# A two-layer transformer kernel: where ScalarE's exponential, roundings and one copy stand in a key-tile loop, and shifts written by four instructions

## The chip, the cores and the metric

The kernel runs on one core of one Trainium2 chip. The metric is device time in microseconds of one execution; the kernel before took 3008.36 us in the median of three runs. TensorE is PE in the profile (PEld is its weight load), VectorE DVE, ScalarE ACT, GpSimd POOL, and SP issues the loads.

## The reference, cut to what matters

Two layers run over x, 32 examples of 64 tokens by 256, with a context of 1601 rows by 256 for each example. Each layer is a cross attention, a self attention and a feed-forward part. The change touches only the second layer's two attentions:

```
kv = (mem @ W_kv).reshape(B, Nkv, 2, HEADS, HEAD_DIM)
k = kv[:, :, 0].transpose(0, 2, 1, 3)
v = kv[:, :, 1].transpose(0, 2, 1, 3)
q = (x @ W_q).reshape(B, Nq, HEADS, HEAD_DIM).transpose(0, 2, 1, 3)
attn = jnp.einsum('bhqd,bhkd->bhqk', q, k) * SCALE
attn = jax.nn.softmax(attn, axis=-1)
out = jnp.einsum('bhqk,bhkd->bhqd', attn, v)
...
return out @ W_proj + b_proj
```

with 16 heads of 16 columns. Then comes a causal self attention with the same heads, computed for two examples (128 tokens) at a time:

```
scores = jnp.where(causal, scores, NEG_INF)
attn = jax.nn.softmax(scores, axis=-1)
out = jnp.einsum('bhst,bhtd->bhsd', attn, V)
...
return scrambled @ W_O
```

## The kernel before, in words

The program goes through four stages: the first layer's attentions (up to some 370 us), its quantized feed-forward part (up to some 625 us), the second layer's attentions (from there to some 2485 us, called the stage here), and an expert feed-forward part. The change lies in the stage.

**Pairs and examples.** The stage runs over 16 pairs of examples. TensorE's program is unrolled over them; ACT, DVE, POOL and SP run the 14 inner pairs as a loop. In pe_batch each example n of a pair has two phases.

*Maxima and projections.* The largest score of each head is needed before any exponential. TensorE makes rounded scores of the example's keys in 16 units (maxima, L1167; unit 0 to 15, two units for each of 8 head pairs), and DVE reduces each to a maximum (L1677). A unit waits until the unit two before it is reduced. Between the units TensorE projects the next example's context to keys (8 pieces, L1145 to L1147) and values (7 pieces, L1154 to L1156), in float32 split into a rounded part and its rest, three products each. ACT copies each key piece out twice, raw and rounded (L780, L781), and POOL subtracts (L550). Behind unit 0 stands the last key tile's weighing of the example before (weigh, L1179), which closes its sums; ACT copies them to SBUF (copy_sums, L835), and behind unit 2 TensorE spreads the denominators (end_batch, L1188), from which DVE takes reciprocals and divides (L1666, L1668). Then the 16 maxima are transposed (L1301), DVE makes two bfloat16 parts of the negated maxima (L1683, L1685) and writes shift, a block pattern on four groups of 8 partitions (L1693), while TensorE does the last three value pieces. The first score matmul (L1317) adds shift and waits for all four groups.

*Scores.* 13 tiles of 128 keys (the last has 65). TensorE makes exact scores of tile t (L1317, L1321) in one of two PSUM halves, ACT takes exponentials (L853), and TensorE weighs the values with them two tiles later, two tiles together (L1179). Tile t waits for the exponentials of tile t - 2.

**What is woven in.** During the scores of a pair, the self attention of the pair before is done beside them, in pieces named by places: place t is tile t of example 0, and place PLACES + t (PLACES is 14) is tile t of example 1. The self attention's 16 heads go in four quarters of four heads. For quarter q TensorE makes scores (L1222), DVE adds the mask, takes maxima and centres (L1702, L1708, L1710), ACT exponentiates (exp_p4, L799), TensorE transposes (L1231), ACT copies the transposed ones out (copy_p4T, L803), TensorE weighs (L1243), DVE copies (L1723), and TensorE transposes back (L1251). The tables S4_AT, EXP_P4_AT, COPY_P4T_AT, P4T_AT, O4_AT and O4T_AT give each quarter's place on its engine. The order on each engine is this hand-written one; an engine that waits holds up everything behind.

ACT also rounds the context of the next example but one (round_ctx, L793), in four parts of 128 x 801 at the tiles of CTX_AT, and POOL makes the rest of each (split_ctx, L558). ctx_raw, the buffer of the raw context, holds half an example's columns (parts 0 and 1, or parts 2 and 3). SP loads the next half (L394) when POOL has finished the two parts of the half before. At tile 7 of example 1, behind parts 2 and 3, ACT copies the normalized x of the next pair (copy_xnT, L691), which TensorE's queries need (L1272, place QUERY_AT[1]).

## Time and profile before

| | us |
|---|---|
| median of 3 runs | 3008.36 (3006.55 to 3012.42) |
| the profiled execution, device time | 3009.89 |
| its span, first to last instruction | 3007.8 |
| PE busy | 2529.8 (84%) |
| PE weight loads busy | 2148.3 (71%) |
| DVE busy | 1612.2 (54%) |
| ACT busy | 1336.3 (44%) |
| POOL busy | 903.5 (30%) |

All rows come from the profiled execution. In a timeline a row is one or several like instructions in order: start, length, engine, line, operation, output<-input, shapes, count, and in brackets the engine's idle time ahead of it with what ended it. A busy PE is a modelled one (matmuls overlap), so where it matters the starts of its rows are compared rather than their ends. "issue" as the end of a wait means that the profile shows nothing that the engine waited for.

### The profile page before, as it was taken

To read this page: it belongs to the slowest core of one execution; us is meant where nothing else is said; L and a number is where in the kernel's file an instruction comes from. 1 tells how busy PE (TensorE), PEld (TensorE's weight loads), DVE (VectorE), ACT (ScalarE), POOL (GpSimd) and SP (SyncE) were. 2 spreads that over 40 slices of the span, in tenths; PEclk is the share of its full clock that TensorE was granted. 3 is DMA by queue.
4 is the path that set the end of the run, shared out by engine and by line. 5 is a ranking of instruction groups with operands and counts; after the bars stand their busy time and mean duration, and the time that the engine had idled before them with its cause. 6 is when DMAs were issued, how large, how long until landed. Compare 5 with 4: busy or idle time off the path is not lost.

```text
span 3007.8 us, 75415 instructions
## 1 busy us (share of the span) xinstructions
PE 2529.8 (84%) x32180; PEld 2148.3 (71%) x32180; DVE 1612.2 (54%) x2741; ACT 1336.3 (44%) x2115; POOL 903.5 (30%) x868
## 2 busy tenths in 40 slices
PE   6999823248999999999999999999999973699997
PEld 3555511137888878888888888888888743699997
DVE  3434377724446456456455455455555543477775
ACT  1212211124555555555555555555555421456564
POOL 1000024344333433442442442443443203211121
PEclk9999955569999999999999999999999975799999
DMA  8888600031010110110110110101101002466664
GB/s 342 323 314 311 235 0 0 0 110 45 24 46 23 35 35 23 35 35 23 35 35 23 35 35 27 43 24 34 35 24 35 2 1 100 159 212 209 209 208 147
DMA packets 48438, 270.05 MB, mean 90 GB/s; under 512 B 4881, under 2 KB 23442, under 8 KB 33554
## 3 DMA queue, kind: packets, MB, share of 16 engines
q1 hardware_dynamic: 40018, 255.69, 23.4%
q0 software_dynamic: 8160, 10.29, 2.2%
q8 instruction: 237, 3.88, 0.5%
q14 instruction: 23, 0.19, 0.0%
HBM read 247.45 MB, written 20.61 MB: 89 GB/s over the span
## 4 chain that ended last, share of the span: by engine, by line
PE 68%; issue 11%; DVE 10%; ACT 6%; POOL 2%; DMA 2%; SPq 0%; ACTq 0%; POOLq 0%; DVEq 0%
PE PS L1321 8%; PE PS L1179 7%; PE PS L1167 5%; PE PS L1317 3%; PE PS L1051 3%; DVE shift L1693 3%; PE PS L1145 3%; PE PS L1147 3%; PE PS L1146 3%; PE PS L1031 3%; PE PS L1408 3%; PE PS L1409 3%; PE PS L1410 3%; PE PS L1156 2%; PE PS L1154 2%
## 5 line engine op out<-in xcount | busy, mean ns | idle before, releaser
L1677 DVE TENSOR_REDUCE mpart<-PS 128x1 f32<-128x802 f32 (+1 forms) x512 | 487.7, 987 | 366.4 <-PE PS L1167 365.1
L853 ACT ACTIVATE probs<-PS 128x1024 f32<-128x1024 f32 (+1 forms) x416 | 413.7, 1026 | 242.2 <-PE PS L1321 242.1
L550 POOL TENSOR_TENSOR k_lo<-probs,k_hi 128x400 fp32r<-128x400 f32 (+1 forms) x256 | 255.7, 999 | 305.0 <-ACT k_hi L781 305.0
L558 POOL TENSOR_TENSOR ctx_lo<-ctx_raw,ctx_hi 128x801 fp32r<-128x801 f32 x128 | 221.8, 1750 | 359.4 <-ACT ctx_hi L793 350.8
L1321 PE MATMUL PS<-qbd_hi,k_hi 64*128 64x256 f32 (+1 forms) x1664 | 313.4, 373 | 0.0
L1167 PE MATMUL PS<-k_hi,qbd_hi 128*128 128x512 f32 (+2 forms) x1024 | 263.3, 359 | 22.4 <-POOL ctx_lo L558 14.2
L780 ACT COPY probs<-PS 128x400 f32<-128x400 f32 (+1 forms) x256 | 126.5, 494 | 305.7 <-PE PS L1147 305.7
L1179 PE MATMUL PS<-probs,vals 128*32 128x64 f32 x13312 | 233.8, 221 | 5.7 <-issue 5.6
L1154 PE MATMUL PS<-wkv_hi,ctx_hi 128*128 128x256 f32 (+1 forms) x832 | 236.4, 284 | 0.0
L1321 PE MATMUL PS<-qbd_lo,k_hi 64*128 64x256 f32 (+1 forms) x1664 | 234.5, 278 | 0.0
L1321 PE MATMUL PS<-qbd_hi,k_lo 64*128 64x256 f32 (+1 forms) x1664 | 234.4, 278 | 0.0
L1156 PE MATMUL PS<-wkv_hi,ctx_lo 128*128 128x256 f32 (+1 forms) x832 | 234.3, 282 | 0.0
L1155 PE MATMUL PS<-wkv_lo,ctx_hi 128*128 128x256 f32 (+1 forms) x832 | 233.2, 280 | 0.0
L1179 PEld LDWEIGHTS PS<-probs,vals 128*32 128x32 f32 x13312 | 196.7, 110 | 45.2 <-issue 28.6
L1167 PEld LDWEIGHTS PS<-k_hi,qbd_hi 128*128 128x128 f32 x1024 | 178.4, 192 | 46.6 <-DVE mpart L1677 24.7
L1408 PE MATMUL PS<-xT_hi,unit_hi 128*128 128x256 f32 x736 | 209.0, 284 | 1.7 <-DVE xT_lo L1920 1.7
L1409 PE MATMUL PS<-xT_lo,unit_hi 128*128 128x256 f32 x736 | 209.3, 284 | 0.0
L1410 PE MATMUL PS<-xT_hi,unit_lo 128*128 128x256 f32 x736 | 208.7, 284 | 0.0
L783 ACT COPY vals<-PS 128x512 f32<-128x512 f32 x192 | 113.0, 589 | 214.3 <-PE PS L1156 214.3
L1145 PE MATMUL PS<-ctx_hi,wkv_hi 128*128 128x400 f32 (+1 forms) x512 | 186.9, 365 | 18.7 <-POOL ctx_lo L558 18.7
L1317 PE MATMUL PS<-shift,onesb 64*128 64x512 bf16 (+1 forms) x832 | 163.8, 390 | 23.5 <-DVE shift L1693 13.5
L664 POOL DMA_INDIRECT sum_d<-scaled,xg x46 | 75.8, 1648 | 346.5 <-DVE scaled L1957 339.5
(322 smaller groups left out, 6088.8 us busy)
## 6 DMA issues: line engine op xcount, KB each, us to landing
unit_raw<-in_experts SPq DMA_DIRECT2D x46, 1536.0 KB, 7.1
ctxN<-in_ctxN SPq DMA_DIRECT2D x16, 3328.0 KB, 10.8
ctxT<-in_ctxT SPq DMA_DIRECT2D x16, 3204.0 KB, 10.4
ctx_raw<-in_ctxT SPq DMA_DIRECT2D x64, 801.0 KB, 4.5
slots_d<-pad_rows SPq DMA_DIRECT2D x2, 2990.0 KB, 18.7
xg<-slots_d SPq DMA_DIRECT2D x23, 260.0 KB, 2.8
x<-in_x SPq DMA_DIRECT2D x1, 2048.0 KB, 9.6
sum_d<-x SPq DMA_DIRECT2D x1, 2048.0 KB, 6.3
```

Of the source, the lines that this page charges most:

```text
L550: g.tensor_tensor(k_lo[:, n, a, c:c + width], k_raw[p % 2][:, 0:width], k_hi[:, n, a, c:c + width].bitcast(F32), ALU.subtract).then_inc(s. ...
L853: act.activation(probs[rows, t % PROBS, :], PS[rows, 1024 * (t % 2):1024 * (t % 2) + 1024], ACT.Exp).then_inc(s.pr_ready, 1)
L1145: pe.matmul(bank(at, width), wkv_hi[:, k, cols], ctx_hi[:, k, c:c + width], start=k == 0, stop=False)
L1154: pe.matmul(to, ctx_hi[:, k, keys], wkv_hi[:, k, D:2 * D], start=k == 0, stop=False)
L1156: mm = pe.matmul(to, ctx_lo[:, k, keys], wkv_hi[:, k, D:2 * D], start=False, stop=k == KT - 1)
L1167: mm = pe.matmul(at, qbd_hi[:, n, pair // 4, (pair % 4) * P:(pair % 4) * P + P], k_hi[:, n, pair // 4, c:c + width], start=True, stop=True)
L1179: mm = pe.matmul(bank(4, S, slice(32 * j, 32 * j + 32), g * S), vals[rows, n, mine:mine + 32], probs[rows, t % PROBS, at_head(h):at_head(h ...
L1321: mm = pe.matmul(bank(2 * (t % 2) + r, 256, rows, a * 256), keys_part[part, n, a, keys], queries[part, n, a, r * 256:r * 256 + 256], start ...
L1408: pe.matmul(to, hi[:, k, cols], tokens_hi[:, k, :], start=k == 0, stop=False)
L1409: pe.matmul(to, hi[:, k, cols], tokens_lo[:, k, :], start=False, stop=False)
L1410: mm = pe.matmul(to, lo[:, k, cols], tokens_hi[:, k, :], start=False, stop=k == KT - 1)
L1677: v.tensor_reduce(mpart[:, pair, half:half + 1], PS[:, at:at + width], AX, ALU.max).then_inc(s.mx_red, 1)
```

## The change

ACT's order in the score loop changes at three points, and DVE's shift instructions are joined. (1) The third quarter's exponential is put at tile 11, in front of the last tile's exponential, instead of behind it; so that the second quarter's copy of transposed exponentials (also at tile 11) does not fall behind it, copies are now issued ahead of exponentials where both stand at one tile. (2) Parts 0 and 1 of the context rounding stood together behind tile 1; part 1 now stands behind tile 3. (3) The copy of the sums stood behind the evacuation of key piece 0 and now stands ahead of it. (4) The shift is written by four instructions of 8 x 512, one for each group of partitions, instead of eight of 8 x 256.

```diff
--- before.py
+++ after.py
@@ -69,11 +69,11 @@
 V_PIECES = [("v", t, min(t + 2, KEY_TILES)) for t in range(0, KEY_TILES, 2)]
 PIECES = K_PIECES + V_PIECES
 PIECE_AFTER = (0, 2, 3, 4, 5, 7, 9, 10, 12, 13, 15)
-CTX_AT = {0: (0, 1), 8: (2,), 10: (3,)}, {0: (0, 1), 6: (2, 3)}
+CTX_AT = {0: (0,), 2: (1,), 8: (2,), 10: (3,)}, {0: (0,), 2: (1,), 6: (2, 3)}
 PROBS = 4
 PLACES = KEY_TILES + 1
 S4_AT = (6, 8, 10, 12)
-EXP_P4_AT = (8, 10, 12, PLACES)
+EXP_P4_AT = (8, 10, 11, PLACES)
 COPY_P4T_AT = (9, 11, 12, PLACES + 3)
 P4T_AT = (8, 10, 12, PLACES + 2)
 O4_AT = (9, 11, 13, PLACES + 3)
@@ -811,10 +811,10 @@
                     act.copy(sqT.rearrange("p k t -> p (k t)"), bank(7, 256)).then_inc(s.sqkv_ready, 1)
                     act.copy(skT.rearrange("p k t -> p (k t)"), bank(7, 256, at=256)).then_inc(s.sqkv_ready, 1)
                     act.copy(v4[:, 0:D], bank(6, 256)).then_inc(s.sqkv_ready, 1)
+                if tile in COPY_P4T_AT:
+                    copy_p4T()
                 if tile in EXP_P4_AT:
                     exp_p4(EXP_P4_AT.index(tile))
-                if tile in COPY_P4T_AT:
-                    copy_p4T()
 
             def prepare(tile):
 
@@ -840,10 +840,10 @@
                         copy_sums()
                     if not (last and b == 1):
                         pieces_evac[0] = 0
-                        for k, piece in enumerate(PIECES):
+                        if not (first and b == 0):
+                            copy_sums()
+                        for piece in PIECES:
                             evac(piece, (b + 1) % 2)
-                            if k == 0 and not (first and b == 0):
-                                copy_sums()
                         T["k_lo"].up(len(K_PIECES))
                     for t in range(KEY_TILES):
                         rows = slice(0, keys_of(t))
@@ -1688,12 +1688,10 @@
                 for r in range(2):
                     for part in range(2):
                         rows = slice(64 * r + 32 * part, 64 * r + 32 * part + PAIRS)
-                        for a in range(KT):
-                            mine = slice(rows.start + 4 * a + 2 * r, rows.start + 4 * a + 2 * r + 2)
-                            ins = v.tensor_tensor(shift[rows, a * 256:a * 256 + 256].rearrange("p (h q) -> p h q", h=2),
-                                                  sh8[rows, part, None, :].broadcast_to([PAIRS, 2, P]),
-                                                  ident[rows, mine, None].broadcast_to([PAIRS, 2, P]), ALU.mult)
-                        ins.then_inc(s.shift_ready, 1)
+                        own_pair = ident[rows, rows.start:rows.start + PAIRS].rearrange("p (a s h) -> p a s h", a=KT, s=2)[:, :, r, :]
+                        v.tensor_tensor(shift[rows, :].rearrange("p (a h q) -> p a h q", a=KT, h=2),
+                                        sh8[rows, part, None, None, :].broadcast_to([PAIRS, KT, 2, P]),
+                                        own_pair[:, :, :, None].broadcast_to([PAIRS, KT, 2, P]), ALU.mult).then_inc(s.shift_ready, 1)
 
             def mask_keys(q):
                 if q >= 2:
```

ACT's program at the last tiles of example 0 in the inner pairs; sideB is the self attention's buffer (L799 is exp_p4, L803 copy_p4T), L853 with 65 rows is tile 12. Difference:

```order
 L853 ACTIVATE probs<-PS 128x1024
 L803 COPY sideB<-PS 128x512
+L798 REGISTER_ALU
+L799 ACTIVATE sideB<-sideB 128x512
 L793 CAST ctx_hi<-ctx_raw 128x801
 L852 REGISTER_ALU
 L853 ACTIVATE probs<-PS 65x1024
-L798 REGISTER_ALU
-L799 ACTIVATE sideB<-sideB 128x512
```

The third quarter's exponential now stands ahead of context part 3 and of tile 12's exponential. The copy of the second quarter stays where it was.

ACT's program at the beginning of the inner loop, where example 0's first key piece is evacuated. Difference:

```order
-L780 COPY probs<-PS 128x402
-L781 CAST k_hi<-PS 128x402
-L834 REGISTER_ALU
 L835 COPY sums<-PS 128x256
+L771 ISA
+L780 COPY probs<-PS 128x402
+L781 CAST k_hi<-PS 128x402
 L771 REGISTER_ALU
```

The copy of the sums moved ahead of both evacuations of piece 0.

ACT's program in example 1 of the inner pairs, from tile 1's exponential on; before:

```order
L853 ACTIVATE probs<-PS 128x1024
L792 REGISTER_ALU
L793 CAST ctx_hi<-ctx_raw 128x801 x2
L852 REGISTER_ALU
L853 ACTIVATE probs<-PS 128x1024
L852 REGISTER_ALU
L853 ACTIVATE probs<-PS 128x1024
L803 COPY sideB<-PS 128x512
```

and now:

```order
L853 ACTIVATE probs<-PS 128x1024
L792 REGISTER_ALU
L793 CAST ctx_hi<-ctx_raw 128x801
L852 REGISTER_ALU
L853 ACTIVATE probs<-PS 128x1024
L852 REGISTER_ALU
L853 ACTIVATE probs<-PS 128x1024
L803 COPY sideB<-PS 128x512
L793 CAST ctx_hi<-ctx_raw 128x801
```

Only one rounding now stands ahead of the fourth quarter's copy; the second follows it. TensorE's and POOL's programs are the same in both kernels.

## Rows read from the trace of the kernel before

**Rows 1.** Busy time by engine, whole two-layer stage; columns: window, length, busy time, granted clock, DMA share, GB/s.
```profile
714.00:2414.00 1700.00, 1603.13 (x25216) 1404.92 (x25214) 897.94 (x1485) 923.98 (x1470) 630.76 (x555) 0.99 0.10 30
```

**Rows 2.** TensorE's waits in the stage, 700 to 2450 us: total, times, longest.
```profile
PE PS L1231 <- ACT sideB L799: 26.1, 42, 1.3
PE PS L1243 <- ACT sideB L803: 16.7, 14, 1.2
PE PS L1188 <- ACT sums L835: 16.3, 31, 0.5
PE PS L1317 <- DVE shift L1693: 13.5, 32, 3.8
...
PE PS L1167 <- DVE mpart L1677: 6.0, 23, 2.4
PE PS L1179 <- issue: 5.6, 5, 2.2
PE PS L1272 <- ACT xnT L691: 2.9, 1, 2.9
```

**Rows 3.** Timeline of PE, tile 12 of example 0.
```profile
1615.88 0.62 PE L1222 MATMUL PS<-sideB 64*128 64x256 f32 x4
1617.77 0.63 PE L1231 MATMUL PS<-ident,sideB 128*128 128x128 f32 x4 [1.27 <-ACT sideB L799]
...
1619.24 0.40 PE L1243 MATMUL PS<-sideB 128*32 128x128 f32 x8
```

**Rows 4.** Timeline of ACT, the same tile.
```profile
1614.05 0.88 ACT L793 CAST ctx_hi<-ctx_raw 128x801 fp32r<-128x801 f32 x1
1616.08 1.02 ACT L853 ACTIVATE probs<-PS 65x1024 f32<-65x1024 f32 x1 [1.15 <-PE PS L1321]
1617.01 0.62 ACT L799 ACTIVATE sideB<-sideB 128x512 f32<-128x512 f32 x1
```

**Rows 5.** Timeline of DVE: centring of the third quarter.
```profile
1614.07 0.69 DVE L1710 TENSOR_TENSOR sideB<-sideB,small 128x512 f32<-128x512 f32 x1
```

**Rows 6.** Timeline of PE, maxima and key projections of the following example.
```profile
1565.45 0.89 PE L1167 MATMUL PS<-k_hi,qbd_hi 128*128 128x512 f32 x4
1566.87 0.70 PE L1188 MATMUL PS<-sums,spread 128*128 128x256 f32 x2 [0.53 <-ACT sums L835]
...
1571.42 0.53 PE L1167 MATMUL PS<-k_hi,qbd_hi 128*128 128x512 f32 x2
...
1575.41 0.63 PE L1167 MATMUL PS<-k_hi,qbd_hi 128*128 128x512 f32 x2 [0.15 <-DVE mpart L1677]
```

**Rows 7.** Timeline of DVE, the same stretch.
```profile
1567.82 1.75 DVE L1666 RECIPROCAL sideB<-PS 128x256 f32<-128x256 f32 x1
...
1569.95 1.88 DVE L1677 TENSOR_REDUCE mpart<-PS 128x1 f32<-128x799 f32 x2
```

**Rows 8.** Timeline of ACT, second example of a pair.
```profile
1540.34 1.62 ACT L793 CAST ctx_hi<-ctx_raw 128x801 fp32r<-128x801 f32 x2
...
1551.30 1.61 ACT L793 CAST ctx_hi<-ctx_raw 128x801 fp32r<-128x801 f32 x2
```

**Rows 9.** Timeline of POOL, the same.
```profile
1541.29 3.76 POOL L558 TENSOR_TENSOR ctx_lo<-ctx_raw,ctx_hi 128x801 fp32r<-128x801 f32 x2 [13.98 <-ACT ctx_hi L793]
```

**Rows 10.** The context loads of the stage (line 394), issue to landing.
```profile
DMA to landing us min/median/max: 4.1/4.5/6.1
```

**Rows 11.** The weight loads' wait for the shift, as in rows 2.
```profile
PEld PS L1317 <- DVE shift L1693: 21.7, 32, 4.1
```

**Rows 12.** DVE by shape: busy us, mean ns, idle before.
```profile
L1693 DVE TENSOR_TENSOR shift<-sh,ident 8x256 bf16<-8x256 bf16 x256 | 96.4, 413 | 4.1
...
L1710 DVE TENSOR_TENSOR sideB<-sideB,small 128x512 f32<-128x512 f32 x64 | 44.3, 692 | 2.2
...
L1668 DVE TENSOR_TENSOR sideB<-sums,sideB 128x256 f32<-128x256 f32 x32 | 13.6, 425 | 1.1
```

**Rows 13.** Timeline of DVE: the eight shift instructions.
```profile
1587.13 3.11 DVE L1693 TENSOR_TENSOR shift<-sh,ident 8x256 bf16<-8x256 bf16 x8
```

## The prediction

> **What bounds the kernel now.** I read the busy times by window first. In 1700 us of the stage TensorE is busy for 1603, at a granted clock of 0.99 of its full 2.4 GHz, and no other engine for more than 924 [rows 1]. So TensorE's program, in the order in which it is written, sets the time, and what an edit elsewhere can give is bounded by TensorE's 97 idle us. The second view is therefore TensorE's list of waits [rows 2]: 26.1 us for the self attention's exponentials, 16.7 for its transposed copies, 16.3 for the copied sums, 13.5 for the shift. The change aims at these four. The third view is the timelines, which tell how much of each wait goes before the next thing is late. They repeat from pair to pair to some hundredths of a us, so one pair stands for all.
>
> **The third quarter's exponential.** At tile 12 of example 0, TensorE makes the fourth quarter's scores (L1222), then stands 1.27 us before the third quarter's transposes at 1617.77 [rows 3]. ACT makes the exponential they need at 1617.01, behind tile 12's own, which started at 1616.08 because it waited for TensorE [rows 4]. The data were ready long before: DVE's centring ended at 1614.07 + 0.69 = 1614.76 [rows 5]. In the new place ACT stands before it from 1614.05, where it now begins context part 3 [rows 4], until 1614.76, and is done at some 1615.4 (0.62 long). Context part 3 (0.88) follows and ends at 1616.2, so tile 12's exponential starts 0.1 us late, and that one is wanted only in the next example. TensorE reaches the transposes at 1617.77 - 1.27 = 1616.5 and finds the exponential ready: all 1.27 us go. What is late next is ACT's copy of the transposed ones. TensorE is done with them near 1617.1 and wants the copy behind one weighing, at 1619.24 - 1.27 = 1617.97 [rows 3]; ACT is free at 1617.1 and its copy is about as long as the exponential, 0.6: ready with 0.2 to 0.3 to spare. POOL's part 3 ends 1.2 us later than now, beside work. It is needed at the start of the next example's maxima, some 2 us behind the transposes, and has about 0.4 us left. There are 15 such places; the 42 waits for L799 [rows 2] are one of these and two of 0.26 us in nearly every pair but the first, and the small ones stay. 15 x 1.26 = **18.9 us**. Bounds: 12 us, if the copy or POOL's part takes 0.4 back, and 20.
>
> **The sums first.** TensorE issues units 1 and 2 from 1565.45, four matmuls at 0.184 us, and could issue the spreading at 1566.18; it does at 1566.87 [rows 6], 0.69 later. The copy's input is ready when the last weighing ends, a whole key piece (1.1 us) earlier, while ACT stands idle; so it costs ACT nothing and TensorE finds it ready. But not all of the 0.69 stays. DVE is busy with units 1 and 2 until 1567.82 in any case, then with the reciprocal and the product until 1569.95, and reduces units 3 and 4 in 1.88 us [rows 7], none of which depends on the copy. Unit 3 is reduced at 1569.95 + 0.99 = 1570.94, and unit 5 waits for that: TensorE issues it at 1571.42 now, could at 1570.73, and will at 1570.98, 0.44 earlier. Unit 9 waits for unit 7. DVE runs units 5 and 6 as fed, and ends unit 7 near 1574.94; TensorE issues unit 9 at 1575.41 now [rows 6] and then at 1574.98, 0.43 earlier. So DVE's reductions take the place of the copy for the rest: 30 examples x 0.43 = **12.9 us**. Bounds: 0.25 (another 0.2 us late at unit 7) and 0.69, or 7.5 and 20.7.
>
> **The roundings apart.** In example 1 both parts, 1.62 us, stand in front of tiles 2 and 3 and of the fourth quarter's copy [rows 8], for which TensorE waits 1.2 us in each of 14 pairs [rows 2]. With one part behind the copy, the copy is 0.75 us earlier (half of the 1.62, less the overlap of one with the next), and 0.4 of the wait stays: 14 x 0.75 = 10.5. In example 0 nothing waits for these exponentials, and the rounding goes in front of tile 4's by 0.1 us: nothing, hidden by the tile order's slack of over 1 us. The price lies in the load. SP's queue loads the second half when POOL has done both first parts, now at 1541.29 + 3.76 = 1545.05 [rows 9]. Part 1 is rounded behind tiles 2 and 3 and the copy, till some 1544.4, so POOL ends near 1546.2, 1.2 us later. A load takes 4.1 to 6.1 us, 4.5 in the median [rows 10]. Now it lands near 1549.7 and ACT wants it at 1551.30 [rows 8]; then it lands near 1550.9 and ACT wants it at 1550.5. ACT waits 0.4 us, and behind it stands the copy of the next pair's x, which has 0.5 us before TensorE wants it: hidden in the median. A load of 5.1 or more shows: I take one in five at 0.6 us, 2 us in all, and 0.5 for the first pair, where TensorE waits 2.9 us for that copy already [rows 2]. **8.2 us**. Bounds: 0 (each of 14 loads costs 0.75) and 11.
>
> **The shift.** Eight instructions, 0.413 us each [rows 12], take 3.11 us [rows 13]: two of a group overlap (0.75 us), and the next group begins 0.03 behind them. No row has a shift of 512, so I bound it: float32 products of 512 and 256 elements take 0.692 and 0.425 [rows 12], 0.267 more for the larger, so a shift of 512 is 0.413 + 0.267 = 0.68. Four with three gaps of 0.03: 2.81, or 0.30 less. In front of the first score matmul TensorE idles (13.5 - 3.8) / 31 = 0.31 us by its matmuls [rows 2], whose ends are modelled, and (21.7 - 4.1) / 31 = 0.57 by its weight loads [rows 11], so nearly all of the 0.30 counts: 32 examples x 0.29 = **9.3 us**. Bounds: 0 (0.75 each, should the three-level operands slow it) and 32 x 0.57 = 18 (should the four overlap as two of a group do).
>
> The Trainium skill (VectorE: DVE Perf Modes, "The DRAIN you can't avoid") says that the next Vector operation does not start until the pipeline has emptied, and advises fewer operations. By it the eight would take 8 x 0.413 + 7 x 0.03 = 3.51 us and the four save 0.70, more than TensorE's 0.57, which would give 18 us in place of 9.3. The trace disagrees: 3.11 for the eight, so there is less to save.
>
> **Sum.** 18.9 + 12.9 + 8.2 + 9.3 = 49.3 us. The profiled execution took 3009.9, so 2960.6 of its kind; it lay 1.5 above the median of 3008.4, for which I forecast **2959 us**, 1.6% less.
>
> **Rivals.**
> *Only the exponential and half the rest.* DVE's reductions swallow the sums' gain (7.5 left), late loads the roundings' (0 left), the shift gives 4: 18.9 + 7.5 + 4 = 30 us, 2978. For it: only 0.4 us of slack at the load and unit 7. Against: the counted slacks are positive in the median.
>
> *The pipeline rule, or more overlap.* Shift 18, sums 16, roundings 10.5, exponential 18.9: 63 us, 2945. For it: the four groups are independent. Against: the 0.03 gap between groups in every example.
>
> *Slower: TensorE's instruction supply.* TensorE stands 5.6 us in 5 places inside a weighing, up to 2.2 us, with nothing to wait for [rows 2]; the program is unrolled, its instructions come by DMA, and the two long stalls lie close behind context loads. If new times made fetches meet loads often, each costs 2.2 us, and more than 49 / 2.2 = 22 further meetings in some 60 loads would make it slower; 30 would give 2959 + 66 = 3025. Against: two long ones in 31 examples, at places that drift, and the change moves loads by 1 us only. The Trainium skill (Runtime: NRT & Kernel Launch, "Instruction fetch mechanics") calls crossing a block of instructions mostly hidden; by it this rival has no price, but the trace has the 2.2.
>
> **How the numbers follow.** Forecast (2950 to 2969): 0.60. Half the rest (2969 to 2984): 0.18. The pipeline rule or more overlap (2941 to 2950): 0.12. Instruction supply: 0.08, spread over gains of 20 us to losses, of which 0.03 end slower and 0.02 within the bound. In 0.02 loads late by far more than the row shows hold it within the bound too. A measurement here can tell 0.2%, 6 us. Faster 0.93, same 0.04, slower 0.03. The range takes in most of the first three: 2944 to 2981.
>
> **What would show it.** TensorE's list: L1231 down from 26.1 to some 7, L1188 gone, L1167 up by 5 to 8, L1243 near 6, L1317 behind the shift near 4 (the last example's), L1272 up a little. Four shift instructions of 0.68 in 2.8 us. Wrong would be: a wait for L799 or L803 at tile 12, waits for L1272 in most pairs, more "issue" waits, or a granted clock below 0.99.

## The result, and the profile after

| | before | after |
|---|---|---|
| median, us | 3010.39 (4 runs, 3006.55 to 3015.33) | 2963.64 (4 runs, 2961.14 to 2965.66) |
| the profiled execution, device time | 3009.89 | 2965.66 |
| its span | 3007.8 | 2963.8 |

The ratio is 0.9843, with a 95% interval from 0.9826 to 0.9861: 46.8 us less by the medians, where 49.3 were forecast. (The median of before includes one run more than the one shown ahead.)

The stage answers to [rows 1]. Busy time by engine in the stage of after; the columns are those of [rows 1]:

```profile
714.00:2370.00 1656.00, 1606.17 (x25250) 1406.97 (x25248) 889.74 (x1372) 926.91 (x1473) 624.70 (x555) 0.99 0.10 31
```

TensorE now idles 50 of 1656 us, where it idled 97 of 1700. It does the same work at the same granted clock, 0.99; only idle time has gone. TensorE's waits in the stage of after answer to [rows 2] (total, times, longest):

```profile
PE PS L1167 <- DVE mpart L1677: 12.7, 55, 2.4
PE PS L1317 <- ACT probs L853: 8.2, 30, 0.7
PE PS L1231 <- ACT sideB L799: 7.5, 28, 0.3
PE PS L1243 <- ACT sideB L803: 6.0, 14, 0.4
PE PS L1272 <- ACT xnT L691: 4.6, 3, 3.1
PE PS L1179 <- issue: 1.9, 3, 0.9
```

The 26.1 us of L1231 became 7.5, the 16.7 of L1243 6.0, the wait for the copied sums (L1188) is gone, and so is the one for the shift, except in the last example, which lies behind this window. L1167, behind DVE's maxima, rose as forecast, and L1272 by 1.7.

**The period.** A good ruler for such a loop is the time from one example's transpose of the maxima (L1301, once per example) to the next. Timeline of PE, these instructions at three successive examples, of before:

```profile
1644.81 0.31 PE L1301 MATMUL PS<-ident,m 128*128 128x128 f32 x1
...
1698.26 0.31 PE L1301 MATMUL PS<-ident,m 128*128 128x128 f32 x1
...
1754.77 0.31 PE L1301 MATMUL PS<-ident,m 128*128 128x128 f32 x1
```

and of after:

```profile
1620.93 0.31 PE L1301 MATMUL PS<-ident,m 128*128 128x128 f32 x1
...
1673.02 0.31 PE L1301 MATMUL PS<-ident,m 128*128 128x128 f32 x1
...
1727.63 0.31 PE L1301 MATMUL PS<-ident,m 128*128 128x128 f32 x1
```

The first distance holds example 1's scores and the second example 0's: 53.45 and 56.51 before, 52.09 and 54.61 after. Each is the commonest value of its kind. Of the fourteen inner pairs' distances of example 1, twelve lie within 0.03 us of it before, but only five within 0.04 in after; the rest are longer, which is taken up below. From the first to the last L1301 the stage took 1702.1 us (711.59 to 2413.68) and now takes 1652.0 (715.54 to 2367.55): 50.1 less. The spans differ by 44.0 only, because the stage began 3.95 us later and the part behind it took 2.1 more. The code ahead of the stage is the same in both. In the thirteen kernels of this document the stage began anywhere from 711.6 to 715.5 us. After's start is the latest of them, but the kernels that are after with one or two more edits began at 712.9 to 714.4, so I read this as scatter, not as a price of the change.

**The places of the forecast.** Timeline of ACT at tiles 11 and 12 of after [rows 4]:

```profile
1594.70 0.63 ACT L799 ACTIVATE sideB<-sideB 128x512 f32<-128x512 f32 x1 [0.62 <-DVE sideB L1708]
1595.24 0.84 ACT L793 CAST ctx_hi<-ctx_raw 128x801 fp32r<-128x801 f32 x1
1595.99 1.02 ACT L853 ACTIVATE probs<-PS 65x1024 f32<-65x1024 f32 x1
```

The third quarter's exponential starts at 1594.70, as soon as DVE has centred it, in front of the rounding (L793) and of tile 12's exponential. Timeline of PE in after: the transposes it feeds, and then the maxima of the following example [rows 3, 6]:

```profile
1596.34 0.66 PE L1231 MATMUL PS<-ident,sideB 128*128 128x128 f32 x4
...
1600.60 0.89 PE L1167 MATMUL PS<-k_hi,qbd_hi 128*128 128x512 f32 x4
1601.33 0.59 PE L1188 MATMUL PS<-sums,spread 128*128 128x256 f32 x2
...
1606.14 0.63 PE L1167 MATMUL PS<-k_hi,qbd_hi 128*128 128x512 f32 x2 [0.20 <-DVE mpart L1677]
...
1613.26 0.90 PE L1167 MATMUL PS<-k_hi,qbd_hi 128*128 128x512 f32 x4
```

The transposes at 1596.34 show no wait, where 1.27 us stood. Units 1 and 2 start at 1600.60 and the spreading at 1601.33 without a wait, where it had 0.53. Timeline of DVE in the same stretch [rows 7], and the new shift [rows 13]:

```profile
1602.97 1.75 DVE L1666 RECIPROCAL sideB<-PS 128x256 f32<-128x256 f32 x1
1604.75 0.44 DVE L1668 TENSOR_TENSOR sideB<-sums,sideB 128x256 f32<-128x256 f32 x1
1605.11 2.77 DVE L1677 TENSOR_REDUCE mpart<-PS 128x1 f32<-128x799 f32 x3
...
1621.93 2.83 DVE L1692 TENSOR_TENSOR shift<-sh,ident 8x512 bf16<-8x512 bf16 x4
```

DVE takes the reciprocal and the product in the same order as before, and they end at 1605.19, with units 3 and 4 behind them. This is what unit 5 now waits 0.20 us for. The four shift instructions take 2.83 us, 0.28 less than the eight.

### The profile page after: what moved, and what is told of

The parts are those of the page before. It is cut to its first block, busy times and chain, and to the rows that moved or that the text cites. A ratio compares the mean times of both kernels' runs of the same rounds, so it can differ in the third digit from the quotient of the medians.

```text
span 2963.8 us, 75287 instructions
## 1 busy us (share of the span) xinstructions
PE 2534.5 (86%) x32180; PEld 2148.2 (72%) x32180; DVE 1599.6 (54%) x2613; ACT 1336.9 (45%) x2115; POOL 897.0 (30%) x868
## 4 chain that ended last, share of the span: by engine, by line
PE 48%; issue 24%; POOL 10%; DVE 9%; ACT 4%; DMA 4%; POOLq 0%; SPq 0%; DVEq 0%; ACTq 0%
PE PS L1321 5%; PE PS L1179 4%; PE PS L1167 3%; POOL k_lo L550 3%; PE PS L1051 3%; POOL ctx_lo L558 3%; PE PS L1031 3%; DVE mpart L1677 2%; PE PS L1317 2%; PE PS L1156 2%; PE PS L1154 2%; PE PS L1155 2%; PE PS L1408 2%; PE PS L1409 2%; PE PS L1410 2%
## 5 line engine op out<-in xcount | busy, mean ns | idle before, releaser
L853 ACT ACTIVATE probs<-PS 128x1024 f32<-128x1024 f32 (+1 forms) x416 | 413.4, 1025 | 207.5 <-PE PS L1321 207.4
L558 POOL TENSOR_TENSOR ctx_lo<-ctx_raw,ctx_hi 128x801 fp32r<-128x801 f32 x128 | 223.0, 1753 | 397.2 <-ACT ctx_hi L793 388.6
L550 POOL TENSOR_TENSOR k_lo<-probs,k_hi 128x400 fp32r<-128x400 f32 (+1 forms) x256 | 248.9, 972 | 263.0 <-ACT k_hi L781 262.9
L1321 PE MATMUL PS<-qbd_hi,k_hi 64*128 64x256 f32 (+1 forms) x1664 | 313.5, 373 | 0.0
L1167 PE MATMUL PS<-k_hi,qbd_hi 128*128 128x512 f32 (+2 forms) x1024 | 265.7, 361 | 29.0 <-POOL ctx_lo L558 14.2
L1321 PE MATMUL PS<-qbd_lo,k_hi 64*128 64x256 f32 (+1 forms) x1664 | 235.4, 279 | 0.7 <-issue 0.6
L1179 PE MATMUL PS<-probs,vals 128*32 128x64 f32 x13312 | 233.8, 221 | 2.0 <-issue 1.9
L1321 PE MATMUL PS<-qbd_hi,k_lo 64*128 64x256 f32 (+1 forms) x1664 | 234.9, 279 | 0.0
L1179 PEld LDWEIGHTS PS<-probs,vals 128*32 128x32 f32 x13312 | 196.8, 110 | 43.6 <-issue 24.7
L1167 PEld LDWEIGHTS PS<-k_hi,qbd_hi 128*128 128x128 f32 x1024 | 175.7, 192 | 62.7 <-DVE mpart L1677 41.0
L1146 PE MATMUL PS<-ctx_lo,wkv_hi 128*128 128x400 f32 (+1 forms) x512 | 178.3, 348 | 0.0
## 6 DMA issues: line engine op xcount, KB each, us to landing
ctxT<-in_ctxT SPq DMA_DIRECT2D x16, 3204.0 KB, 10.5
```

The source lines that it names most:

```text
L550: g.tensor_tensor(k_lo[:, n, a, c:c + width], k_raw[p % 2][:, 0:width], k_hi[:, n, a, c:c + width].bitcast(F32), ALU.subtract).then_inc(s. ...
L558: g.tensor_tensor(ctx_lo[:, a, cols], ctx_raw[:, cols], ctx_hi[:, a, cols].bitcast(F32), ALU.subtract).then_inc(s.ctx_lo_ready, 1)
L853: act.activation(probs[rows, t % PROBS, :], PS[rows, 1024 * (t % 2):1024 * (t % 2) + 1024], ACT.Exp).then_inc(s.pr_ready, 1)
L1167: mm = pe.matmul(at, qbd_hi[:, n, pair // 4, (pair % 4) * P:(pair % 4) * P + P], k_hi[:, n, pair // 4, c:c + width], start=True, stop=True)
L1179: mm = pe.matmul(bank(4, S, slice(32 * j, 32 * j + 32), g * S), vals[rows, n, mine:mine + 32], probs[rows, t % PROBS, at_head(h):at_head(h ...
L1321: mm = pe.matmul(bank(2 * (t % 2) + r, 256, rows, a * 256), keys_part[part, n, a, keys], queries[part, n, a, r * 256:r * 256 + 256], start ...
```

## The experiments

Times are medians, each with its ratio to the kernel before and the 95% interval. "us less" for a part alone is what the ratio takes off the 3011 us that the kernel before took beside it. "Period" is the commonest distance between two L1301, as above.

### Each part alone

Four kernels each make one part of the change, in the kernel before. The edit of the first, without anything else of the change:

```diff
-EXP_P4_AT = (8, 10, 12, PLACES)
+EXP_P4_AT = (8, 10, 11, PLACES)
...
-                if tile in EXP_P4_AT:
-                    exp_p4(EXP_P4_AT.index(tile))
                 if tile in COPY_P4T_AT:
                     copy_p4T()
+                if tile in EXP_P4_AT:
+                    exp_p4(EXP_P4_AT.index(tile))
```

> Edit to the kernel before: only the third quarter's exponential at tile 11, copies ahead of exponentials. Theory (each part gives what its own wait left after the next late thing, and the parts add up): the 1.27 us wait for L799 goes in 15 pairs, nothing takes its place, 19 us less, ratio 0.9937; the time from transpose to transpose of the maxima (L1301) of an example 0 falls from 56.5 to 55.25 us, that of an example 1 stays at 53.45. Rival (ACT's copy at tile 12 or POOL's part 3 is late next): 0.4 us or more comes back as a wait for L803 or L558 in each pair, 13 us or less.

Measured: 2989.14 us, ratio 0.9933 (0.992 to 0.9945), 20.2 us less. TensorE's waits in its stage:

```profile
PE PS L1243 <- ACT sideB L803: 16.6, 14, 1.2
...
PE PS L1231 <- ACT sideB L799: 7.3, 27, 0.3
...
PE PS L1179 <- issue: 0.9, 2, 0.7
```

L1231 fell by 18.8 and nothing took its place; L1243 is that of before. The period of example 0 went from 56.51 to 55.17, that of example 1 stayed. The "issue" stalls at L1179 are 0.9 us here, against 5.6 before, though nothing in this edit touches TensorE's instructions; what they are is taken up with the rivals below.

The second has only the sums' copy in front of piece 0:

```diff
-                        for k, piece in enumerate(PIECES):
+                        if not (first and b == 0):
+                            copy_sums()
+                        for piece in PIECES:
                             evac(piece, (b + 1) % 2)
-                            if k == 0 and not (first and b == 0):
-                                copy_sums()
```

> Edit to the kernel before: only the copy of the sums ahead of key piece 0. Theory (DVE's reductions are late next): the wait of L1188 goes, TensorE's wait for L1677 appears at unit 5 (0.2 us by the matmuls) and 0.43 to 0.46 us of 0.69 stay for each of 30 examples: both periods 0.45 shorter, 13 us less, ratio 0.9957. Rival (the copy alone was the limit): no wait at unit 5, 0.69 each, 21 us. Rival (DVE gives nothing): 0.

Measured: 3001.64 us, 0.9965 (0.9952 to 0.9978), 10.5 us less. The periods fell by 0.36 and 0.33, where 0.45 was expected. Its wait for DVE's maxima:

```profile
PE PS L1167 <- DVE mpart L1677: 12.5, 54, 2.4
```

L1188 has no wait left, and L1167 rose from 5.8 to 12.5 in 54 places (its 5.8 of before are those of the stage alone): DVE's units took back part of it.

The third separates the roundings only:

```diff
-CTX_AT = {0: (0, 1), 8: (2,), 10: (3,)}, {0: (0, 1), 6: (2, 3)}
+CTX_AT = {0: (0,), 2: (1,), 8: (2,), 10: (3,)}, {0: (0,), 2: (1,), 6: (2, 3)}
```

> Edit to the kernel before: only the context parts 0 and 1 apart. Theory: the period that holds example 1's scores falls by 0.75 us in 14 pairs, the wait for L803 falls from 1.2 to 0.43; late loads show as a wait for L1272 of at most 1.5 us in one to four pairs and the first pair waits 0.2 to 0.5 us more: 7 to 10 us less, ratio 0.997. Rival (the later load costs every pair): a wait for L1272 in most pairs, nothing gained.

Measured: 3004.39 us, 0.9976 (0.9965 to 0.9986), 7.2 us less. Its waits:

```profile
PE PS L1243 <- ACT sideB L803: 6.0, 14, 0.4
...
PE PS L1272 <- ACT xnT L691: 4.2, 3, 3.2
```

L1243 fell by 10.7, the 14 x 0.75 that was forecast, and L1272 rose by 1.3. Example 1's shortest periods are 0.78 less, but they spread from 52.67 to 54.23, where twelve of before's fourteen lie within 0.03; in the mean they fell by 0.52, 7.3 us in 14 pairs.

The fourth writes the shift by four instructions:

```diff
-                        for a in range(KT):
-                            mine = slice(rows.start + 4 * a + 2 * r, rows.start + 4 * a + 2 * r + 2)
...
+                        own_pair = ident[rows, rows.start:rows.start + PAIRS].rearrange("p (a s h) -> p a s h", a=KT, s=2)[:, :, r, :]
+                        v.tensor_tensor(shift[rows, :].rearrange("p (a h q) -> p a h q", a=KT, h=2),
```

> Edit to the kernel before: only the shift in four instructions. Theory: 2.83 us for the four in place of 3.11, and TensorE's first score matmul 0.28 us earlier in each of 32 examples: 9 us less, ratio 0.997. Rival (the gap in front of it has another cause): less than 3 us, with a gap of 0.2 to 0.3 left in front of L1317.

Measured: 2999.49 us, 0.9962 (0.9949 to 0.9975), 11.4 us less. Both periods fell by 0.28, 8.7 us in 31 examples, and the four instructions take 2.82 us.

The four gains add up: 20.2 + 10.5 + 7.2 + 11.4 = 49.3 us by the ratios, each uncertain by 3 to 4 us. That this is the very number of the forecast is luck. The periods, which scatter less, say the same: example 0's fell by 1.34 + 0.36 + 0.02 + 0.28 = 2.00 apart and by 1.90 together, example 1's by 0.33 + 0.78 + 0.28 = 1.39 apart and 1.36 together. So to 0.1 us per example the parts neither feed on each other nor get in each other's way.

### Does DVE start the next instruction before the last has ended?

The rival that gave the shift 18 us rests on an answer of no. This kernel is before with its eight shift instructions in another order, so that each works on another group of partitions than the one ahead:

```diff
-                for r in range(2):
-                    for part in range(2):
+                for a in range(KT):
+                    for r in range(2):
+                        for part in range(2):
...
-                        for a in range(KT):
...
-                        ins.then_inc(s.shift_ready, 1)
+                            if a == KT - 1:
+                                ins.then_inc(s.shift_ready, 1)
```

> Edit to the kernel before: the same eight shift instructions, but all four groups of partitions for the first half of the columns, then all four for the second, so that no instruction follows one on the same group; semaphores on the last four. Theory (an instruction on another group of partitions starts only when the one before has ended): no two overlap, 8 x 0.413 + 7 x 0.03 = 3.5 us in place of 3.11, TensorE's wait in front of L1317 0.4 us longer in 32 examples, 12 us slower than before. Rival (the gap of 0.03 came from the semaphore increment): the first four overlap, 3.11 us or less, same time.

Measured: 3024.37 us, 1.0044 (1.0027 to 1.0061), 13 us more. Timeline of its DVE:

```profile
1592.67 3.47 DVE L1693 TENSOR_TENSOR shift<-sh,ident 8x256 bf16<-8x256 bf16 x8
```

and TensorE's wait for it in the stage, where before had 9.7 us:

```profile
PE PS L1317 <- DVE shift L1693: 21.3, 31, 0.7
```

Eight of the same instructions take 3.47 us in this order, and 3.11 where two of a group follow each other [rows 13]. One takes 0.417 us here, so 8 x 0.417 = 3.34 and the seven gaps come to 0.14: none overlaps. By the starts and ends in the trace, 0.01 us lie behind each of the first four, which raise no semaphore, and 0.03 behind the others, which do. So the semaphore makes the gap longer, as the second theory had it, but it does not bring the overlap back: the overlap is there where the group stays the same, and is lost where it changes. The 0.36 us show nearly whole in the period (56.89 and 53.83, 0.38 more).

### What the load costs when the rounding is still later

After, with part 1 of example 1 behind tile 5:

```diff
-CTX_AT = {0: (0,), 2: (1,), 8: (2,), 10: (3,)}, {0: (0,), 2: (1,), 6: (2, 3)}
+CTX_AT = {0: (0,), 2: (1,), 8: (2,), 10: (3,)}, {0: (0,), 4: (1,), 6: (2, 3)}
```

> Edit to the kernel after the change: in example 1, context part 1 behind tile 5 in place of tile 3, another two tiles (3 us) later. Theory (the load's slack is used up by the change): POOL ends part 1 about 3 us later, the load of the second half lands 3 us later, ACT waits at tile 7, and TensorE's wait for L1272 appears in all 14 pairs with 2 to 3 us, so 25 to 45 us more than the changed kernel, the upper end if the clock drops behind those waits. Rival (there was slack left, the rounding can stand anywhere in the first six tiles): no wait for L1272 but in the first pair, the same time as the changed kernel.

Measured: 3040.69 us, 1.0101 (1.0084 to 1.0118): 77 us more than after and 29 more than before, well beyond the 25 to 45 that were expected. TensorE's wait for the copy of x in its stage:

```profile
PE PS L1272 <- ACT xnT L691: 50.4, 15, 3.6
```

That is 45.8 us more than in after, 3.3 in each pair where 2 to 3 were expected. The rest lies behind each wait. Timeline of PE at one of them, and the windows around it (the third number from the end is the granted clock):

```profile
1344.55 0.80 PE L1272 MATMUL PS<-xnT,w_cq 128*128 128x128 f32 x2 [3.51 <-ACT xnT L691]
```

```profile
1336.00:1341.00 5.00, 5.00 (x106) 4.04 (x104) 1.60 (x6) 1.96 (x2) 2.60 (x3) 1.00 0.38 118
...
1344.50:1350.50 6.00, 5.95 (x75) 5.34 (x79) 0.00 (x0) 2.25 (x4) 4.99 (x5) 0.57 0.41 134
1350.50:1360.00 9.50, 9.50 (x259) 8.23 (x249) 2.01 (x3) 4.84 (x7) 5.88 (x4) 1.00 0.02 5
```

TensorE stands 3.51 us, and then works for 6 us at a granted clock of 0.57, close to the lower of its two levels, 1.2 GHz; ahead of the wait it had 2.4 GHz, and it has it again behind 1350.5. By an estimate 6.0 x (1 - 0.57) = 2.6 us are lost, and example 1's period grew by 5.9 (52.09 to 57.95), which is the 3.3 of the wait and these 2.6. In the mean it is 5.4 in 14 pairs and 3.5 in the first, 79 us of stage. The load chain is thus as near to the edge as the prediction had it: two tiles earlier it costs 1.7 us of TensorE's waits in all, here it costs every pair.

### Earlier exponentials for the other quarters

L1231 still has 7.5 us in after, two small waits in nearly every pair. After, with the first and second quarters' exponentials one tile earlier:

```diff
-EXP_P4_AT = (8, 10, 11, PLACES)
+EXP_P4_AT = (7, 9, 11, PLACES)
```

> Edit to the kernel after the change: the first and second quarters' exponentials also in front of the tile's exponential, at tiles 7 and 9 in place of 8 and 10. Theory: the two waits of 0.26 us for L799 in each of 15 pairs go and nothing is late next: 8 us less than the changed kernel, no wait for L799 left in inner pairs. Rival (ACT, which now waits for DVE's centring in front of a tile's exponential, makes TensorE wait for that tile): L1317 waits for L853 in example 0, no gain or a loss of up to 10 us.

Measured: 2963.55 us, 0.984 (0.9823 to 0.9856), no different from after's 2963.64. TensorE's wait at L1243 in its stage:

```profile
PE PS L1243 <- ACT sideB L803: 9.8, 29, 0.4
```

8 us less was expected. L1231 has no wait left, and L1243 has 15 new ones and 3.8 us more. Timeline of its ACT:

```profile
1585.88 0.63 ACT L799 ACTIVATE sideB<-sideB 128x512 f32<-128x512 f32 x1 [1.59 <-DVE sideB L1708]
1586.41 1.92 ACT L853 ACTIVATE probs<-PS 128x1024 f32<-128x1024 f32 x2
1588.22 0.59 ACT L803 COPY sideB<-PS 128x512 f32<-128x512 f32 x1
```

The copy that L1243 waits for (L803) stands behind two exponentials of tiles in one piece, 1586.41 to 1588.33; the exponential that was moved (L799) had idled ACT for DVE's centring, and delayed both. So 0.26 us of wait before one instruction became a wait before the next. The second quarter's gain went too, at another place. Timeline of PE in the same example:

```profile
1595.00 0.70 PE L1222 MATMUL PS<-sideB 64*128 64x256 f32 x4
```

By the starts in the trace, these scores of the fourth quarter begin 0.26 us later after the matmuls ahead of them than in after, 0.05 us behind the end of DVE's copy (L1721), which they wait for. Example 0's period is 54.71 in place of 54.61. Neither theory had foreseen either.

### The reciprocal in two halves

What remains at L1167 is DVE's reciprocal and product between units 2 and 3. After, with the reciprocal in halves behind units 2 and 10 (divide_half takes half the columns) and the product behind unit 13:

```diff
...
-                    if u == 2 and not (first and b == 0):
-                        end_batch(1 - b)
+                    if not (first and b == 0):
+                        if u == 2:
+                            v.wait_ge(s.den_ps, T["den"].up())
+                        if u in (2, 10):
+                            divide_half(1 - b, 0 if u == 2 else 1)
+                        if u == 13:
+                            v.wait_ge(s.vec_step, T["step"].now())
+                            mine = attn4[:, :, (1 - b) * S:(2 - b) * S]
+                            v.tensor_tensor(mine, sums_sb[:, :].rearrange("p (g q) -> p g q", g=4), mine, ALU.mult).then_inc(s.attn_ready, 1)
```

> Edit to the kernel after the change: DVE's reciprocal of the sums in two halves, behind units 2 and 10, and the product behind unit 13, in place of all three steps behind unit 2. Theory (this block of 2.1 us on DVE is what took the place of the copy): TensorE's wait at unit 5 goes, that at unit 9 stays or shrinks, 0.25 to 0.45 us less in each of 30 examples, 8 to 13 us less than the changed kernel. Rival (the waits at units 5 and 9 come from the reductions themselves): no change, or slower by the extra instruction.

Measured: 2947.7 us, 0.9787 (0.9771 to 0.9803), 16 us below after, where 8 to 13 were expected; the stage is 14.4 us shorter. Timeline of its DVE:

```profile
1593.37 0.95 DVE L1672 RECIPROCAL sideB<-PS 128x128 f32<-128x128 f32 x1
...
1603.20 0.95 DVE L1672 RECIPROCAL sideB<-PS 128x128 f32<-128x128 f32 x1
```

and TensorE's wait for the maxima:

```profile
PE PS L1167 <- DVE mpart L1683: 5.7, 24, 1.1
```

A half takes 0.95 us, the whole took 1.75 [rows 7]. The same work, spread out, leaves TensorE fewer waits at the maxima: L1167 fell from 12.7 to 5.7, and the two periods fell by 0.49 and 0.48. Instruction by instruction, this lies at unit 5 alone: its first matmul starts 0.36 us earlier than in after, measured from the matmuls ahead of it, and the second another 0.11. So the wait that the profile lists there with 0.20 us cost 0.47. This shows that what swallowed a part of the sums' gain is DVE's reciprocal and product between units 2 and 3.

### The copy of x ahead of its part

Three kernels ask whether after's spread of example 1's periods comes from late loads. In after ACT waits for the load of the second half in nearly every pair, where before had one such wait of 1.3 us. ACT's waits in the stage of after:

```profile
ACT ctx_hi L793 <- DMA ctx_raw<-in_ctxT: 8.6, 14, 1.6
```

The first kernel is after with the copy of the next x between context parts 2 and 3:

```diff
-                    copy_xnT(7)
...
                                     round_ctx(part)
+                                    if b == 1 and part == 2:
+                                        copy_xnT(7)
```

> Edit to the kernel after the change: at tile 7 of example 1 ACT copies the next pair's x between context parts 2 and 3 instead of behind both. Theory (the spread of the periods that hold example 1's scores, 52.1 to 53.2 us, comes from late loads that hold ACT in front of this copy): TensorE's waits for L1272, 4.6 us in 3 places and smaller ones unlisted, shrink, 12 of 14 periods lie within 0.2 of 52.1, and it is 4 to 9 us faster than the changed kernel, 2 to 3 of it in the first pair. Rival (POOL's parts and the queries, now 0.4 us later, are late next at the next pair's first example): a wait of L1167 for the queries L563, no gain or a loss.

Measured: 2959.63 us, 0.9833 (0.9819 to 0.9846), within the uncertainty of after. Its waits (its line numbers are one higher behind the edit):

```profile
PE PS L1273 <- ACT xnT L691: 4.2, 2, 4.0
...
PE PS L1180 <- issue: 3.3, 4, 1.2
```

Of the two late waits of the middle pairs one of 0.2 us is left, but the first pair's wait is 4.0 us, where after had 3.1, since part 2 itself waits for the load there (ACT stands 3.1 us for it, where it stood 1.5); and the periods spread as in after, from 52.05 to 53.57, with 3.3 us of stalls at L1180 for which the waits name no cause. My expectation, that waits for the copy of x make most of the spread, was wrong. Comparing the pairs of after instruction by instruction shows what it is made of: over 52.09 the fourteen periods have 5.8 us, of which 1.9 stand at L1272, in four pairs, and nearly all the rest at single matmuls of L1179 and L1321.

The next is the same with the halved reciprocal:

> The halved reciprocals and the copy of x between the parts, both on the kernel after the change. Theory (the two gains are at different places and add up): 15 to 16 us and 4 to 9 us less than the changed kernel, 2938 to 2944 us. Rival: the earlier examples take the load's slack again, and the second gain stays under 3 us, 2945 or more.

Measured: 2943.39 us, 0.978 (0.9765 to 0.9794). That is 4 us below halves and 20 below after; the copy's own 4 us lie within the uncertainty both times.

The last puts the copy ahead of both parts, with the halved reciprocal:

```diff
                             if t % 2:
+                                if b == 1 and t == 7:
+                                    copy_xnT(7)
                                 for part in CTX_AT[b].get(t - 1, ()):
                                     round_ctx(part)
```

> As the kernel best, with the copy of the next pair's x ahead of both context parts at tile 7 of example 1. Theory (in the first pair and with the slowest loads ACT stands before part 2 for the load, in front of the copy): TensorE's waits for ACT's copy at the queries go in all pairs, 2.5 to 3.5 us less than best, most of it in the first pair. Rival (parts 2 and 3 end 0.4 to 2 us later, POOL's query products behind them are late at the next example): a wait of L1167 for the query products in most pairs, slower than best.

Measured: 2940.54 us, 0.977 (0.9756 to 0.9784), 23 us below after and 71 below before: the lowest median of all, though not clear of the last kernel's. TensorE's waits of its stage:

```profile
PE PS L1318 <- ACT probs L852: 8.6, 31, 0.7
PE PS L1232 <- ACT sideB L799: 7.4, 28, 0.3
PE PS L1244 <- ACT sideB L803: 6.1, 14, 0.4
PE PS L1168 <- DVE mpart L1684: 4.8, 20, 1.1
...
PE PS L1168 <- POOL ctx_lo L558: 0.9, 1, 0.9
...
PE PS L1168 <- POOL qbd_lo L563: 0.4, 1, 0.4
```

No wait for the copy of x is left. The first pair's example 1 takes 48.0 us in place of 52.2, part of which is the clock: behind after's wait of 3.1 us there, it reads 0.72 over the 6 us from 781.0. ACT waits for the load once, 1.4 us. TensorE's two waits for POOL's results (0.9 and 0.4 us, once each) cost a little; the first, for L558, is 0.9 with the halved reciprocal alone as well. And the spread has nearly gone: twelve of the fourteen periods lie within 0.2 us of 51.61, and all have 2.2 us over it, where the kernel ahead has 5.8 and an L1180 with 2.7 us of stalls in place of 1.2. So where ACT stands for the load does bear on the spread, but by the stalls and not by the waits for the copy.

## Why the prediction was right

**What bounds it.** From the first L1301 to the last, TensorE is busy for 1605.2 us before and 1604.2 after, while the stage is 50.1 shorter. So the gain is idle time of TensorE and next to nothing else. All its listed waits come to 94.6 us before and 44.4 after, 50.2 less. That this fits so well is in part luck, since a listed wait is shorter than what it costs, as the next terms show.

**The exponential, 18.9 us.** The waits fell by 18.6 in after and 18.8 alone; 15 x 1.34 = 20.1 by the period, 20.2 by the medians. The step that reads "ready with 0.2 to 0.3 to spare" for ACT's copy held: no wait for L803 at that tile. The term was a little low, and the period's 20.1 lies on its upper bound of 20. The difference, 0.07 us per place, stands at the same instruction: the first transpose starts 1.33 us earlier after the matmuls ahead of it, where the list, which counts from the modelled end of the one before, has 1.27.

**The sums, 12.9 us.** The mechanism was right and the size too large: 0.36 and 0.33 per example, 10.4 us. From unit 1 to unit 5 TensorE took 5.97 us and takes 5.54 (1606.14 less 1600.60): 0.43 less, as forecast (0.44). But only unit 5's first matmul is so much earlier. Behind a wait the second starts 0.34 us after the first, and 0.23 where there is none, so the two of unit 5 are 0.63 us long now (1606.14) and were 0.53 [rows 6]. The forecast left these 0.10 us out. Unit 6 is then issued 0.33 earlier, DVE ends unit 7 0.08 us later than I had worked out from its rows, and unit 9, forecast at 0.43, starts 0.33 earlier. (The wait for the sums in before had cost 0.10 more than the forecast's 0.69 in the same way, so the copy gave 0.79 us and unit 5 took 0.46 of it back.) It stays so. Timeline of PE of before, unit 11:

```profile
1578.46 0.90 PE L1167 MATMUL PS<-k_hi,qbd_hi 128*128 128x512 f32 x4
```

From unit 1 to this one it took 13.01 us (1578.46 less 1565.45), in after 12.66 (1613.26 less 1600.60): 0.35. The kernel with the halved reciprocal shows the cause in another way: with DVE's reciprocal out of its way, unit 5 has neither the wait nor the wider pair, 0.47 us in all.

**The roundings, 8.2 us.** The waits at L1243 fell by 10.7, forecast 10.5. The late loads cost 1.7 us at L1272 in after (1.3 alone), forecast 2.5. So 9.0 us by the waits, 7.2 (4.2 to 10.5) by the medians of the part alone. ACT's wait of 0.4 us for the load, forecast for the median pair, is there: 0.2 to 1.6 us in thirteen of the fourteen inner pairs, 0.3 in their middle. What I had not foreseen is the spread of example 1's periods: it is more than the late loads explain. Over their commonest values the inner pairs' periods of after, of both kinds, have 7.2 us in excess, of which some 1.9 are late loads (two of the four too short for the list); those of before 8.4, at fewer and longer stalls.

**The shift, 9.3 us.** 0.28 in each of 31 examples, 8.7, and 0.2 in the last example's. 11.4 (7.5 to 15.4) by the medians. One instruction takes 0.683 us, estimated 0.68, and four 2.83, estimated 2.81.

**The rivals.** *Half the rest* falls, since all three smaller parts gave more than that each; its time would have been 2978. *The pipeline rule, or more overlap*, 2945, falls by the time and by its largest term: the shift alone gave 11.4 us (7.5 to 15.4), not 18. (Its 16 us for the sums stand in the forecast without a working.) The rule itself, in the wording of the Trainium skill (VectorE: DVE Perf Modes, "The DRAIN you can't avoid"), falls by the rows of before, 3.11 us, beside those of the interleaved shifts. I had left out the last sentence of that section, by which an operation that is not held starts earlier. The section of the Trainium skill that it points to (same page, "Two Vector instructions with no wait between them") holds an instruction whose input or output starts in another group of 32 partitions than the one before: by that rule, eight interleaved ones all wait (3.51 us) and two of one group overlap. The runs agree with it, at 3.47 and 3.11. *The instruction supply* made nothing slower. Its stalls come to 5.6 us at L1179 before, 1.9 after, 0.9 with the exponential alone and 6.9 with the shift alone, while TensorE's program is the same in all. With those at L1317 and L1321 they come to 7.1 before and 3.6 after, so up to 3.5 of the 46.8 us gained is theirs. The rival's mechanism, though, is there in the traces. DMA queues of before, in the 3.1 us up to 1508.10, while a load of the context runs:

```profile
q1 hardware_dynamic: 130, 0.81, 84.4%
```

and in the 2.4 us from there to 1510.50, in which TensorE's longest such stall lies:

```profile
q8 instruction: 1, 0.02, 2.5%
```

The stages of the thirteen kernels have 198 such instruction packets of 16 KB each, and 69 stalls of over 0.15 us between them. All 69 end 2.1 to 2.8 us after an instruction packet started, and in 67 of them at least 40 packets of a load had been under way in the 2 us ahead of that packet. Of the 568 instruction packets that met a load in this way one in eight is followed by a stall, and of the other 2006 two are. Whose instructions a packet brings the traces do not say. But the stalls come back at the same place of TensorE's program: one at the same matmul of L1317 in all thirteen kernels (1053.7 in before, 1049.2 in after), one at the same of L1179 in eleven (1118.4 and 1111.6). The one of 1.95 us at 1622.80 stands at the same matmul in all five kernels that have the third quarter's exponential at its old place, with 1.8 to 2.1 us, and in none of the eight that have it at the new one. So the traces speak for fetches of instructions that meet a context load, one profile of each kernel; no run was made to move these stalls on purpose.

Together: 20.1 + 10.4 + 9.0 + 8.7 = 48.2 by periods and waits, and 50.1 in the stage, where the fewer stalls cover the difference; 49.3 had been forecast. The mechanism of each term held. That the sum came within 1.1 us is in part luck: the exponential and the roundings were taken too low by 1.2 and 0.8, the sums too high by 2.5 and the shift by 0.6.

## What to carry to other kernels

Where one engine's program sets the time, count each of its waits by what would be late next, and follow that one step further: the terms then add up, and each edit can be priced from one repetition. An edit that takes a wait away at one instruction may give it to the next in the same program, if both wait for the same engine; so it is the distance between repetitions that shows a gain, and not the wait that has gone. The wait as it is listed can be too small as well: 0.20 us in the list cost 0.47 here. And where a transfer lands with half a microsecond to spare, work in front of what releases it should not be moved again without counting anew. Two tiles more cost 77 us here, not the 25 to 45 that had been expected: 46 in waits, and most of the rest because the clock fell behind each.

## What the runs showed of the hardware

- TensorE's granted clock after a wait of 3.5 us: 0.57 over the 6 us behind it, a loss of 2.6 us by an estimate, which none of its waits shows. Behind the wait of 2.9 us in the first pair of before (ending at 778.38) it reads 0.72 over 6 us, behind its longest stall without a named cause (2.2 us, ending at 1510.47) 1.00 in the next 3 us, and behind a wait of 2.4 us in its last example (ending at 2400.27) 0.50 over 6 us.
- TensorE's second matmul behind a wait starts 0.34 us after the first, and 0.23 without a wait (units of 128x512 in before and after). So a wait listed with 0.20 us cost 0.47.
- DVE overlaps two instructions on the same 32 partitions by 0.07 us (two of 0.413 in 0.75); on different ones by nothing, and 0.01 us lie between them, or 0.03 where the first raises a semaphore. An order that changes partitions each time cost 13 us here.
- TensorE's stalls without a named cause, 0.2 to 2.2 us each, came to 1 to 8 us per kernel in the stage. All 69 of the thirteen kernels end 2.1 to 2.8 us after a 16 KB packet of the instruction queue started, 67 of them after one that met a context load. They are as large as the smallest part of this change: a part worth under 4 us can't be told from them by the time of one profiled execution, but by the periods.
